# Layer two's edge pass: four row updates per step become one scan over features and columns

## The chip, the cores and the metric

The kernel runs on one core of one Trainium2 chip. The metric is the device time of one execution in microseconds (us), the median of the runs shown. A step of the work is followed on five engines: TensorE (PE, with PEld for its weight loads), VectorE (DVE), ScalarE (ACT), GpSimd (POOL) and SyncE (SP, which only issues DMAs). Each engine takes its instructions strictly in the order of the program; between engines only semaphores order anything.

## The reference, cut to what matters

Four graph layers run one after the other over 50000 nodes with 256 features and 25000 edges sorted by target node. After each layer its result is added to the node features and a layer norm is taken. The change is in the third of them, which the code calls layer two (L2): attention over the incoming edges of a node, with 8 heads of 32 features.

```python
def _L2_gnn_ref(feat, src, dst, W, attn_l, attn_r):
    ft = (feat @ W).reshape(n, H, D)
    a1 = jnp.einsum('nhd,hd->nh', ft, attn_l)
    a2 = jnp.einsum('nhd,hd->nh', ft, attn_r)
    e = jax.nn.leaky_relu(a1[src] + a2[dst], negative_slope=ALPHA)
    m = jax.ops.segment_max(e, dst, num_segments=n)
    ex = jnp.exp(e - m[dst])
    s = jax.ops.segment_sum(ex, dst, num_segments=n)
    alpha = ex / s[dst]
    msg = ft[src] * alpha[:, :, None]
    out = jax.ops.segment_sum(msg, dst, num_segments=n)
    return jax.nn.elu(out.reshape(n, H * D))
...
x = _layernorm(x + _L2_gnn_ref(x, src, dst, L2_gnn_W, L2_gnn_attn_l, L2_gnn_attn_r), axis=-1)
```

## The kernel before

The program has six phases with a barrier after each: layer zero's edges, two passes over the nodes, layer two's edge pass (the functions `e2_...`), layer three's edge pass, and a last pass over the nodes. The change touches layer two's edge pass alone.

There the sorted edges are cut into 128 runs of 196, one run per partition, and the pass goes through the runs column by column, J = 4 columns to a step, CS = 49 steps. Each partition so keeps, from column to column, a running maximum, a running sum and a running weighted mean (the row, 256 features) of the edges of its current target node; at the first edge of a new node they start afresh. Column j of a step does row = al * previous row + B, where al is one factor per head and B is the column's own message.

All loops are unrolled, and what stands where on each engine is the order of the code, written out by hand:

- **TensorE** (`e2_tensor`): for each column four transposes (L1356) of source and target features into one PSUM bank, then matmuls with the layer's weights (L1367, L1369). The transposes of a column wait for the ScalarE copy that frees their bank, two columns earlier; the matmuls wait for ScalarE's copy of their own column.
- **ScalarE** (`e2_scalar`), per step s: `ev` (L1402) copies the transposes of step s+1 out of PSUM, two columns, then `ex` (L1407, exponentials of the weights of step s), then the two other columns of `ev`; then `normed` of step s-1 (L1426, four instructions, the normalised rows that are stored), `tail` (L1412, the running sum and maximum into the row's last columns), and `relu_exp` (L1417 Relu, L1419 Exp, 1024 elements each), which needs the step's rows.
- **VectorE** (`e2_vector`), per step s: `chain(s)` (L1506 to L1526, thirteen short instructions on scores and maxima), `settle(s-1)` (L1533 to L1549: the ELU, the residual and the layer-norm statistics of the step before, which needs the Exp of `relu_exp(s-1)`), `sums_rows(s)`: the running sum, a reciprocal, the factors `cf2`; B for two columns at a time (L1565) with the factor al2 between them (L1569); then for each column al * previous row (L1578), a fill of the target features (L1582) and the sum with B (L1586). Each row waits for the row before it.
- **GpSimd** gathers source rows, scatters results, and works out the layer norm's scale (`rstd`) between them. **SyncE** loads target rows, stores the rows (`raw_store`, L1279) and the results.

So a step's rows go from VectorE to ScalarE (`relu_exp`) and back (`settle`), and ScalarE's copies `ev` go to TensorE and back.

Of the kernel before, what the change touches and what calls it, by code (L numbers as in the profile page):

```python
# [94 lines left out]
def gnn_program(nc, x, src, dst, ea256, ea64,  # L95
# [62 lines left out]
    with ctx:  # L158
# [1037 lines left out]
        def scan(v, out, a, c, op0, op1):  # L1196
# [10 lines left out]
        xT2 = take([2, 4, P])  # L1207
        row2 = take([NG, J, TW])
        un2 = take([J, D])
        rr2 = take([2, J, D])  # L1210
        y2 = take([NG, J, D])
        tB2 = take([J, D])
        adx2 = take([2, H2, J + 1])
# [7 lines left out]
        cf2 = take([2, H2, J])  # L1221
        al2 = take([H2, J])
        st2 = take([J, 6])
# [21 lines left out]
        e2 = {k: Signal(sem(f"e2_{k}")) for k in  # L1245
              ("tab", "rowd", "zero", "head", "hrow", "ev", "chain", "eL", "M", "d", "w", "s", "tail", "cf", "B", "A", "S", "xc",
               "mn", "ex", "u", "r", "nm", "end", "spread", "top", "wx", "wT", "old", "z", "wf", "new", "fix", "fixed")}
# [13 lines left out]
        def e2_sync(sp):  # L1261
# [14 lines left out]
            def raw_store(s):  # L1276
                wait(sp, e2["S"], J * (s + 1))
                wait(sp, e2["tail"], s + 1)
                sp.dma_start(raws_v[s, :, :, :], row2[:, s % NG, :, :]).then_inc(e2_rw[s % NG].sem, 16)  # L1279
# [118 lines left out]
        def e2_scalar(act):  # L1398
# [29 lines left out]

            wait(act, e2["zero"], 5)
            for j in range(J):  # L1430
                ev(0, j)
            for s in range(CS):
                for j in range(J):
                    if j == J // 2:
                        ex(s)
                    if s + 1 < CS:
                        ev(s + 1, j)
                if s > 0:
                    normed(s - 1)
                tail(s)  # L1440
                wait(act, e2["S"], J * (s + 1))
                relu_exp(s, row2[:, s % NG, :, 0:D], un2, s)
            wait(act, e2["top"], 3)
# [11 lines left out]
        def e2_vector(v):  # L1455
            t = [0]

            def link(ins):
                t[0] += 1
                ins.then_inc(e2["tab"].sem, 1)  # L1460
                wait(v, e2["tab"], t[0])
            for a in (row2[:, NG - 1, J - 1, :], adx2, ee2, ms2, ww2):
                v.memset(a, 0.0).then_inc(e2["zero"].sem, 1)
# [33 lines left out]
            v.memset(KEEP3[:, CS - 1, :, 1], 0.0).then_inc(e2["rowd"].sem, 1)  # L1497
            wait(v, e2["zero"], 5)

# [28 lines left out]
            def settle(s):  # L1528
                c, b = s % NG, s % 2
                wait(v, e2["ex"], s + 1)  # L1530
                wait(v, e2["S"], J * (s + 1))
# [19 lines left out]
            def sums_rows(s):  # L1551
                b, c = s % 2, s % NG
                w1, w2 = ww2[:, 2 * b, :, :], ww2[:, 2 * b + 1, :, :]
                sums = ms2[:, b, 0, :, :]
                wait(v, e2["w"], s + 1)
                scan(v, sums, w1, w2, ALU.mult, ALU.add).then_inc(e2["s"].sem, 1)
                wait(v, e2["s"], s + 1)
                wait(v, e2["S"], J * s)
                v.reciprocal(inv2, sums[:, :, cur]).then_inc(e2["cf"].sem, 1)
                wait(v, e2["cf"], 3 * s + 1)  # L1560
                v.tensor_tensor(out=cf2, in0=ww2[:, 2 * b:2 * b + 2, :, cur],
                                in1=inv2.rearrange("p (a h) j -> p a h j", a=1).to_broadcast([P, 2, H2, J]), op=ALU.mult).then_inc(e2["cf"].sem, 1)
# [7 lines left out]
                wait(v, e2["cf"], 3 * s + 3)  # L1570
                wait(v, e2_rw[c], 16 * (s // NG))
                if s > 0:
                    wait(v, e2["r"], s)
# [628 lines left out]
```

## Time and profile before

| | |
|---|---|
| runs | 5112.55, 5115.06, 5118.44 us; median 5115.06 us |
| profiled execution | 5112.93 us, span 5111.2 us |
| busy over the span | PE 4226.6 us (83%), DVE 3516.5 us (69%), ACT 1963.0 us (38%), POOL 3216.0 us (63%) |
| layer two's edge pass, 3274 to 3980 us | DVE busy 633.87 us of 706, PE 503.98, POOL 481.13, ACT 326.77 |
| mean granted TensorE clock | 0.904 of full speed over the span, 0.75 in this pass |

The profile is one execution. A row of the timeline gives the start and the duration of an instruction (or of several alike, merged), and in brackets how long its engine had been idle before it and what ended that. Two instructions that follow each other on an engine overlap a little, so what one costs is best read from start to start. TensorE's clock is given as a share of its higher level: 1.00 is 2.4 GHz and 0.50 is 1.2 GHz.

### The profile page before, as it was taken

The page shows a single profiled execution, that of the slowest core. Times are in us where ns is not written, and L with a number is a line of the kernel's source. Part 1 is how long each engine was busy: PE and PEld are TensorE (multiplying, and loading weights), DVE is VectorE, ACT ScalarE, POOL GpSimd, SP SyncE. Part 2 cuts the span into 40 slices and gives each one's busy share as a digit, 9 for nine tenths or more (in the row PEclk, how much of TensorE's full clock was granted, in tenths as well). Part 3 has the DMA queues.
Part 4 walks back from the last instruction along what each step waited for, and adds up shares of the span by engine and source line. Part 5 has one row for each costly group of instructions (what it writes and reads, how often), then busy time and mean ns, then how long its engine had stood idle before and what let it go on. Part 6 is the DMA issues. An engine that isn't in the chain of part 4 may idle for free. (4 is left out here: it accounts for less than half of the span.)

```text
span 5111.2 us, 69926 instructions
## 1 busy us (share of the span) xinstructions
PE 4226.6 (83%) x18336; PEld 3066.5 (60%) x18336; DVE 3516.5 (69%) x10200; ACT 1963.0 (38%) x3445; POOL 3216.0 (63%) x3078
## 2 busy tenths in 40 slices
PE   2177759998999999999999999777776687768886
PEld 1055535555666666666666666566665677756665
DVE  3055545666666666666666666599999688879998
ACT  0011115553333333333333333344444222237776
POOL 7388754444456666666655656677775677756666
PEclk6588879999999999999999999877777788889999
DMA  9988879998544444444444444355554444448886
GB/s 373 324 157 153 161 141 362 364 367 312 198 175 152 142 143 144 142 140 140 148 142 141 141 141 146 111 183 183 194 183 162 136 140 134 154 166 288 289 288 220
DMA packets 449380, 994.26 MB, mean 195 GB/s; under 512 B 147560, under 2 KB 230474, under 8 KB 449198
## 3 DMA queue, kind: packets, MB, share of 16 engines
q1 hardware_dynamic: 296146, 732.73, 42.1%
q0 software_dynamic: 100736, 172.47, 13.4%
q10 hardware_dynamic: 52316, 87.06, 5.0%
q8 instruction: 62, 1.02, 0.1%
q14 instruction: 120, 0.98, 0.1%
HBM read 493.48 MB, written 541.33 MB: 202 GB/s over the span
## 5 line engine op out<-in xcount | busy, mean ns | idle before, releaser
L1140 PE MATMUL psum<-W2b,arena 128*128 128x256 f32 x3136 | 725.2, 379 | 0.0
L1121 PE MATMUL psum<-arena,W1b 128*128 128x512 f32 x1568 | 699.1, 599 | 0.0
L1140 PEld LDWEIGHTS psum<-W2b,arena 128*128 128x128 f32 x3136 | 573.1, 190 | 66.3 <-issue 0.5
L1121 PEld LDWEIGHTS psum<-arena,W1b 128*128 128x128 f32 x1568 | 289.8, 190 | 402.8 <-issue 402.8
L1009 ACT ACTIVATE arena<-psum,hbias 128x512 f32<-128x512 f32 x392 | 269.4, 687 | 565.3 <-PE psum L1121 565.3
L1367 PE MATMUL psum<-Wg,arena 128*128 128x264 f32 x784 | 299.6, 520 | 167.5 <-ACT arena L1402 166.7
L825 DVE TENSOR_SCALAR arena<-arena 128x256 f32<-128x256 f32 x392 | 135.4, 409 | 424.8 <-POOL arena L820 424.8
L959 POOL DMA_INDIRECT xd_d<-arena,FE x360 | 356.3, 990 | 99.4 <-issue 99.4
L464 POOL DMA_INDIRECT tab<-arena x196 | 310.7, 1585 | 168.6 <-DMA tab<-zero 68.6
L816 POOL TENSOR_TENSOR arena<-arena,lneps 128x4 f32<-128x4 f32 x196 | 41.5, 212 | 549.2 <-DVE arena L812 548.3
L603 PE MATMUL psum<-arena,NEG 128*128 128x324 f32 x500 | 177.3, 521 | 245.1 <-ACT arena L409 212.5
L1097 PE MATMUL psum<-W2a,arena 128*128 128x256 f32 x1568 | 357.1, 381 | 9.3 <-ACT arena L995 9.3
L2025 PE MATMUL psum<-Wg,arena 128*128 128x256 f32 x1568 | 355.4, 380 | 0.8 <-ACT arena L2041 0.8
L1097 PEld LDWEIGHTS psum<-W2a,arena 128*128 128x128 f32 x1568 | 299.6, 191 | 92.5 <-issue 54.3
L778 PE MATMUL psum<-arena,W1a 128*128 128x512 f32 x784 | 354.1, 595 | 0.0
L728 POOL DMA_INDIRECT fe_d<-EID,FIRST x196 | 196.4, 1002 | 239.6 <-ACT arena L753 209.3
L2084 POOL TENSOR_TENSOR arena<-arena 128x1024 f32<-128x1024 f32 x98 | 230.4, 2351 | 164.1 <-DVE arena L2125 159.6
L939 POOL TENSOR_TENSOR arena<-arena,b2b 128x1024 f32<-128x1024 f32 x98 | 230.7, 2354 | 157.0 <-DVE arena L1078 154.0
L1071 DVE TENSOR_TENSOR arena<-arena 128x4 f32<-128x4 f32 x98 | 214.4, 2188 | 149.3 <-issue 146.5
L409 ACT ACTIVATE arena<-psum 128x324 f32<-128x324 f32 x196 | 71.5, 446 | 632.1 <-DMA tab<-arena 579.6
L2025 PEld LDWEIGHTS psum<-Wg,arena 128*128 128x128 f32 x1568 | 290.9, 191 | 36.8 <-ACT arena L2041 1.2
L1367 PEld LDWEIGHTS psum<-Wg,arena 128*128 128x128 f32 x784 | 182.2, 257 | 205.4 <-ACT arena L1402 178.2
(349 smaller groups left out, 10167.0 us busy)
## 6 DMA issues: line engine op xcount, KB each, us to landing
arena<-in_x SPq DMA_DIRECT2D x194, 512.0 KB, 5.4
x_d<-arena SPq DMA_DIRECT2D x194, 512.0 KB, 3.7
tab<-zero SPq DMA_DIRECT2D x11, 5832.0 KB, 54.3
arena<-x_d SPq DMA_DIRECT2D x105, 512.0 KB, 4.4
tab<-blank SPq DMA_DIRECT2D x97, 544.0 KB
arena<-tab SPq DMA_DIRECT2D x97, 544.0 KB
h_d<-arena SPq DMA_DIRECT2D x98, 512.0 KB, 4.7
arena<-h_d SPq DMA_DIRECT2D x98, 512.0 KB
```

The source lines that it names most:

```text
L464: pool.indirect_dma_start(out=tab0[:, :], out_offset=bass.IndirectOffsetOnAxis(ap=sidx[:, s, j:j + 1], axis=0), in_=comb[:, s % NC, j, :], ...
L778: last = pe.matmul(psum[:, 4 + 2 * b + g, :], W1a[:, f, g * P:(g + 1) * P], hT[:, b, f, :], start=(f == 0), stop=(f == FH - 1))
L939: pool.tensor_tensor(out=x1b[:, k.b, :, :], in0=x1[:, k.b, :, :], in1=b2b[:, :].rearrange("p (a d) -> p a d", a=1).to_broadcast([P, J, D]) ...
L959: pool.indirect_dma_start(out=xd_d[:, :], out_offset=bass.IndirectOffsetOnAxis(ap=FE[:, s * J + j:s * J + j + 1], axis=0), in_=x2[:, s % 2 ...
L1009: act.activation(hid[:, c, :], psum[:, HB[c], :], ACT.Relu, bias=hbias[:, c:c + 1]).then_inc(p3["hidr"], 1)
L1071: v.tensor_tensor(out=lone[:, 0, :], in0=lnB.mv[:, :, 1], in1=lnB.rs, op=ALU.mult).then_inc(lonely["lvar"], 1)
L1097: last = pe.matmul(outA(j), p3y[:, f, j * P:(j + 1) * P], W2a[:, f, :], start=(f == 0), stop=(f == FH - 1))
L1121: last = pe.matmul(psum[:, HB[c], :], W1b[:, f, c * P:(c + 1) * P], x1T[:, f, :], start=False, stop=(f == FH - 1))
L1140: last = pe.matmul(outB(j), hid[:, c, j * P:(j + 1) * P], W2b[:, c, :], start=(c == 0), stop=(c == KH - 1))
L1367: pe.matmul(o[:, 0:D + H2], xT2[:, j % 2, f, :], Wg[2][:, f, 0:D + H2], start=(f == 0), stop=(f == FH - 1))
L2025: done = pe.matmul(psum[:, c + j // 2, (j % 2) * D:(j % 2 + 1) * D], l_xT[:, k.slot(2), f, j * P:(j + 1) * P], Wg[3][:, f, 0:D], start=(f ...
L2084: pool.tensor_tensor(out=l_rr[:, k.slot(4), :, :], in0=l_pr[:, k.slot(2), :, :], in1=l_xt[:, k.slot(NXT), :, :], op=ALU.add).then_inc(lp[" ...
```

## The change

The four rows of a step are no longer made by eight VectorE instructions but by one scan, `tensor_tensor_scan`, over 256 features times 5 columns: along each feature it computes state = al * state + B. Column 0 holds the previous step's last row (copied there by L1582 of the new file) with the factor zero, which starts each feature afresh. Rows now lie as features x columns in a new tile run2 (two buffers, five elements = 20 bytes from one feature to the next), and B is written in that layout too. Since a scan reads a factor for every element, ScalarE spreads the 8 x 5 factors over 8 x 32 x 5 (`spread`, 1280 elements); and since the store wants rows as columns x features, ScalarE copies them back into row2 after `relu_exp` (1024 elements). `relu_exp` and `settle` read run2 with a stride of 20 bytes. The fill of the target features stays: two of its four instructions stand ahead of the scan, two behind it. `raw_store` and the pass's last row wait for ScalarE's copy (signal raw) instead of the row updates.

```diff
+            def spread(s):
+                wait(act, e2["cf"], 3 * s + 3)
+                wait(act, e2["S"], s)
+                act.activation(al5.rearrange("p (h c) j -> p h c j", h=H2), al2.rearrange("p h (a j) -> p h a j", a=1).to_broadcast([P, H2, D // H2, J + 1]),
+                               ACT.Copy).then_inc(e2["A"].sem, 1)
...
                 if s > 0:
                     normed(s - 1)
+                spread(s)
                 tail(s)
-                wait(act, e2["S"], J * (s + 1))
-                relu_exp(s, row2[:, s % NG, :, 0:D], un2, s)
+                wait(act, e2["S"], s + 1)
+                relu_exp(s, run2[:, s % 2, :, 1:J + 1].rearrange("p d j -> p j d"), un2, s)
+                wait(act, e2_rw[s % NG], 16 * (s // NG))
+                act.activation(row2[:, s % NG, :, 0:D], run2[:, s % 2, :, 1:J + 1].rearrange("p d j -> p j d"), ACT.Copy).then_inc(e2["raw"].sem, 1)
...
-                v.scalar_tensor_tensor(out=rr2[:, b, :, :], in0=un2, scalar=-1.0, in1=row2[:, c, :, 0:D], op0=ALU.add, op1=ALU.max).then_inc(e2["u"].sem, 1)
+                v.scalar_tensor_tensor(out=rr2[:, b, :, :], in0=un2, scalar=-1.0, in1=run2[:, b, :, 1:J + 1].rearrange("p d j -> p j d"), op0=ALU.add, op1=ALU.max).then_inc(e2["u"].sem, 1)
...
+                wait(v, e2["A"], s)
+                v.tensor_tensor(out=al2[:, :, cur], in0=cf2[:, 0, :, :], in1=sums[:, :, last], op=ALU.mult).then_inc(e2["cf"].sem, 1)
                 for h in range(2):
-                    v.tensor_tensor(out=tB2[:, 2 * h:2 * h + 2, :].rearrange("p j (h c) -> p j h c", h=H2),
+                    v.tensor_tensor(out=tB2[:, :, 1 + 2 * h:3 + 2 * h].rearrange("p (h c) j -> p j h c", h=H2),
...
-                    if h == 0:
-                        v.tensor_tensor(out=al2, in0=cf2[:, 0, :, :], in1=sums[:, :, last], op=ALU.mult).then_inc(e2["cf"].sem, 1)
...
+                v.tensor_copy(tB2[:, :, 0], run2[:, 1 - b, :, J]).then_inc(e2["B2"].sem, 1)
                 wait(v, e2["mm"], J * (s + 1))
                 for j in range(J):
-                    prev = row2[:, c, j - 1, 0:D] if j else row2[:, (c - 1) % NG, J - 1, 0:D]
-                    wait(v, e2["S"], J * s + j)
-                    v.tensor_tensor(out=split(row2[:, c, j, 0:D], H2), in0=split(prev, H2), in1=heads(al2[:, :, j], H2), op=ALU.mult).then_inc(e2["A"].sem, 1)
...
-                    wait(v, e2["A"], J * s + j + 1)
-                    wait(v, e2["B"], 2 * s + j // 2 + 1)
-                    v.tensor_tensor(out=row2[:, c, j, 0:D], in0=row2[:, c, j, 0:D], in1=tB2[:, j, :], op=ALU.add).then_inc(e2["S"].sem, 1)
+                    if j == 1:
+                        wait(v, e2["A"], s + 1)
+                        wait(v, e2["B"], 2 * s + 2)
+                        wait(v, e2["B2"], s + 1)
+                        wait(v, e2["raw"], s - 1)
+                        wait(v, e2["ex"], s - 1)
+                        v.tensor_tensor_scan(out=run2[:, b, :, :].rearrange("p d j -> p (d j)"), data0=al5.rearrange("p d j -> p (d j)"),
+                                             data1=tB2.rearrange("p d j -> p (d j)"), initial=0.0, op0=ALU.mult, op1=ALU.add).then_inc(e2["S"].sem, 1)
...
-            wait(v, e2["S"], J * CS)
+            wait(v, e2["raw"], CS)
```

On ScalarE, in the middle of the pass, one step before (L1402 is `ev`, L1407 `ex`, L1426 `normed`, L1412 `tail`, L1417 and L1419 `relu_exp`):

```order
L1402 ACTIVATE arena<-psum 128x512 x2
L1407 ACTIVATE arena<-arena 128x16x4
L1402 ACTIVATE arena<-psum 128x512 x2
L1426 ACTIVATE arena<-arena 128x256 x4
L1412 ACTIVATE arena<-arena 128x2x4x8
L1417 ACTIVATE arena<-arena 128x1024
L1419 ACTIVATE arena<-arena 128x1024
```

The same step of the changed kernel (L1404 is `ev`, L1409 `ex`, L1435 `normed`, L1415 `spread`, L1421 `tail`, L1426 and L1428 `relu_exp`, L1454 the copy into row2):

```order
L1404 ACTIVATE arena<-psum 128x512 x2
L1409 ACTIVATE arena<-arena 128x16x4
L1404 ACTIVATE arena<-psum 128x512 x2
L1435 ACTIVATE arena<-arena 128x256 x4
L1415 ACTIVATE arena<-arena 128x1280
L1421 ACTIVATE arena<-arena 128x2x4x8
L1426 ACTIVATE arena<-arena 128x1024
L1428 ACTIVATE arena<-arena 128x1024
L1454 ACTIVATE arena<-arena 128x4x256
```

The new `spread` stands behind all four `ev` and behind `normed`; the new copy stands between the Exp and the next step's first `ev`.

On VectorE, `sums_rows` of one step before, from the factors cf2 (L1561) to the first instructions of the next `chain` (L1506); the group L1578, L1582, L1586 comes four times in a row and is shown once:

```order
L1561 TENSOR_TENSOR arena<-arena 128x64
L1565 TENSOR_TENSOR arena<-psum,arena 128x512
L1569 TENSOR_TENSOR arena<-arena 128x32
L1565 TENSOR_TENSOR arena<-psum,arena 128x512
L1578 TENSOR_TENSOR arena<-arena 128x256
L1582 SCALAR_TENSOR_TENSOR arena<-arena,KEEP 128x256
L1586 TENSOR_TENSOR arena<-arena 128x256
...
L1506 COPY arena<-psum 128x8x2 x2
```

The same stretch of the changed kernel (L1573 is cf2, L1577 al2, L1579 the two B, L1582 the copy of the previous row, L1588 the fill of the target features, L1596 the scan, L1518 the next `chain`):

```order
L1573 TENSOR_TENSOR arena<-arena 128x64
L1577 TENSOR_TENSOR arena<-arena 128x8x4
L1579 TENSOR_TENSOR arena<-psum,arena 128x2x256 x2
L1582 COPY arena<-arena 128x256
L1588 SCALAR_TENSOR_TENSOR arena<-arena,KEEP 128x256 x2
L1596 SCALAR_TENSOR_TENSOR arena<-arena 128x1280
L1588 SCALAR_TENSOR_TENSOR arena<-arena,KEEP 128x256 x2
L1518 COPY arena<-psum 128x8x2 x2
```

The factor al2 moved ahead of both B, and the scan, which waits for ScalarE's `spread`, took the place of the eight row instructions.

## Rows read from the trace of the kernel before

**Rows 1.** Waits, 3300 to 3900 us: engine line <- releaser: total us, times, longest
```profile
ACT arena L1417 <- DVE arena L1586: 67.0, 44, 2.8
...
DVE arena L1533 <- ACT arena L1419: 18.6, 44, 0.4
```

**Rows 2.** Timeline of ScalarE, a late step: start us, us, engine, line, what [idle before]
```profile
3921.06 1.06 ACT L1417 ACTIVATE arena<-arena 128x1024 f32<-128x1024 f32 x1 [1.81 <-DVE arena L1586]
3922.14 1.06 ACT L1419 ACTIVATE arena<-arena 128x1024 f32<-128x1024 f32 x1
3923.11 1.06 ACT L1402 ACTIVATE arena<-psum 128x512 f32<-128x512 f32 x2
...
3930.17 0.60 ACT L1402 ACTIVATE arena<-psum 128x512 f32<-128x512 f32 x1 [2.07 <-PE psum L1356]
3930.66 2.06 ACT L1426 ACTIVATE arena<-arena 128x256 f32<-128x256 f32 x4
3932.63 0.30 ACT L1412 ACTIVATE arena<-arena 128x64 f32<-128x64 f32 x1
3934.76 1.06 ACT L1417 ACTIVATE arena<-arena 128x1024 f32<-128x1024 f32 x1 [1.83 <-DVE arena L1586]
```

**Rows 3.** Timeline of VectorE, one step in the middle of the pass
```profile
3512.70 1.22 DVE L1533 SCALAR_TENSOR_TENSOR arena<-arena 128x1024 f32<-128x1024 f32 x1 [0.43 <-ACT arena L1419]
...
3519.45 0.41 DVE L1578 TENSOR_TENSOR arena<-arena 128x256 f32<-128x256 f32 x1
...
3519.78 0.48 DVE L1582 SCALAR_TENSOR_TENSOR arena<-arena,KEEP 128x256 f32<-128x256 f32 x1
...
3524.10 0.25 DVE L1506 COPY arena<-psum 128x16 f32<-128x16 f32 x2
...
3525.77 0.19 DVE L1526 TENSOR_TENSOR arena<-arena,NEG 128x32 f32<-128x32 f32 x1
...
3526.39 1.23 DVE L1533 SCALAR_TENSOR_TENSOR arena<-arena 128x1024 f32<-128x1024 f32 x1 [0.43 <-ACT arena L1419]
```

**Rows 4.** Timeline of ScalarE: first and last `ev` of two early steps
```profile
3293.62 1.06 ACT L1402 ACTIVATE arena<-psum 128x512 f32<-128x512 f32 x2
...
3299.67 0.60 ACT L1402 ACTIVATE arena<-psum 128x512 f32<-128x512 f32 x1 [1.13 <-PE psum L1356]
...
3320.98 1.06 ACT L1402 ACTIVATE arena<-psum 128x512 f32<-128x512 f32 x2
...
3328.69 0.60 ACT L1402 ACTIVATE arena<-psum 128x512 f32<-128x512 f32 x1 [2.75 <-PE psum L1356]
```

**Rows 5.** Busy time by stretch: us, PE, PEld, DVE, ACT, POOL busy (instructions), PEclk, DMA
```profile
3294.20:3297.60 3.40, 3.34 (x12) 2.94 (x13) 3.33 (x6) 0.64 (x3) 0.00 (x0) 0.52 0.01 2
3297.60:3301.00 3.40, 3.00 (x19) 2.54 (x18) 3.22 (x16) 1.93 (x4) 2.27 (x3) 0.97 0.00 0
...
3325.00:3328.40 3.40, 3.40 (x14) 2.99 (x13) 3.20 (x16) 0.60 (x1) 2.26 (x3) 0.50 0.09 33
```

**Rows 6.** Groups of VectorE instructions by shape, scans: count | busy us, mean ns | idle
```profile
L1198 DVE TENSOR_TENSOR_SCAN arena<-arena 128x20 f32<-128x20 f32 x98 | 19.3, 197 | 1.7
...
L1198 DVE TENSOR_TENSOR_SCAN arena<-NEG,arena 128x40 f32<-128x40 f32 x49 | 11.8, 241 | 1.7
L1198 DVE TENSOR_TENSOR_SCAN arena<-arena 128x40 f32<-128x40 f32 x49 | 11.5, 234 | 0.3 <-ACT arena L1407 0.3
...
L1198 DVE TENSOR_TENSOR_SCAN arena<-NEG,arena 128x20 f32<-128x20 f32 x49 | 9.9, 201 | 4.4
```

**Rows 7.** Groups of ScalarE instructions by shape: count | busy us, mean ns | idle
```profile
L1417 ACT ACTIVATE arena<-arena 128x1024 f32<-128x1024 f32 x49 | 51.8, 1056 | 79.6 <-DVE arena L1586 79.6
...
L1412 ACT ACTIVATE arena<-arena 128x64 f32<-128x64 f32 x49 | 15.0, 306 | 0.0
L1801 ACT ACTIVATE arena<-arena 128x48 f32<-128x48 f32 x49 | 14.2, 289 | 85.9 <-DVE arena L1198 85.9
L1407 ACT ACTIVATE arena<-arena 128x64 f32<-128x64 f32 x49 | 12.5, 256 | 0.7 <-DVE arena L1526 0.7
```

More of the change, by code:

```diff
@@ L1208, in gnn_program @@
         row2 = take([NG, J, TW])
+        run2 = take([2, D, J + 1])
+        al5 = take([D, J + 1])
+        tB2 = take([D, J + 1])
         un2 = take([J, D])
@@ L1211, in gnn_program @@
         y2 = take([NG, J, D])
-        tB2 = take([J, D])
         adx2 = take([2, H2, J + 1])
@@ L1221, in gnn_program @@
         cf2 = take([2, H2, J])
-        al2 = take([H2, J])
+        al2 = take([H2, J + 1])
         st2 = take([J, 6])
@@ L1245, in gnn_program @@
         e2 = {k: Signal(sem(f"e2_{k}")) for k in
-              ("tab", "rowd", "zero", "head", "hrow", "ev", "chain", "eL", "M", "d", "w", "s", "tail", "cf", "B", "A", "S", "xc",
+              ("tab", "rowd", "zero", "head", "hrow", "ev", "chain", "eL", "M", "d", "w", "s", "tail", "cf", "B", "A", "S", "xc", "raw", "B2",
                "mn", "ex", "u", "r", "nm", "end", "spread", "top", "wx", "wT", "old", "z", "wf", "new", "fix", "fixed")}
@@ L1276, in raw_store @@
             def raw_store(s):
-                wait(sp, e2["S"], J * (s + 1))
+                wait(sp, e2["raw"], s + 1)
                 wait(sp, e2["tail"], s + 1)
@@ L1427, in normed @@
                                    scale=rs2[:, s % 2, j:j + 1]).then_inc(e2["y"].sem, 1)
-            wait(act, e2["zero"], 5)
+            wait(act, e2["zero"], 6)
             for j in range(J):
@@ L1461, in link @@
                 wait(v, e2["tab"], t[0])
-            for a in (row2[:, NG - 1, J - 1, :], adx2, ee2, ms2, ww2):
+            for a in (run2[:, 1, :, J], al2, adx2, ee2, ms2, ww2):
                 v.memset(a, 0.0).then_inc(e2["zero"].sem, 1)
@@ L1497, in e2_vector @@
             v.memset(KEEP3[:, CS - 1, :, 1], 0.0).then_inc(e2["rowd"].sem, 1)
-            wait(v, e2["zero"], 5)
+            wait(v, e2["zero"], 6)
             def chain(s):
@@ L1530, in settle @@
                 wait(v, e2["ex"], s + 1)
-                wait(v, e2["S"], J * (s + 1))
+                wait(v, e2["S"], s + 1)
                 wait(v, e2["y"], J * (s - 1))
-                v.scalar_tensor_tensor(out=rr2[:, b, :, :], in0=un2, scalar=-1.0, in1=row2[:, c, :, 0:D], op0=ALU.add, op1=ALU.max).then_inc(e2["u"].sem, 1)
+                v.scalar_tensor_tensor(out=rr2[:, b, :, :], in0=un2, scalar=-1.0, in1=run2[:, b, :, 1:J + 1].rearrange("p d j -> p j d"), op0=ALU.add, op1=ALU.max).then_inc(e2["u"].sem, 1)
                 wait(v, e2["u"], s + 1)
@@ L1557, in sums_rows @@
                 wait(v, e2["s"], s + 1)
-                wait(v, e2["S"], J * s)
+                wait(v, e2["S"], s)
                 v.reciprocal(inv2, sums[:, :, cur]).then_inc(e2["cf"].sem, 1)
                 wait(v, e2["cf"], 3 * s + 1)
-                v.tensor_tensor(out=cf2, in0=ww2[:, 2 * b:2 * b + 2, :, cur],
-                                in1=inv2.rearrange("p (a h) j -> p a h j", a=1).to_broadcast([P, 2, H2, J]), op=ALU.mult).then_inc(e2["cf"].sem, 1)
+                v.tensor_tensor(out=cf2, in0=ww2[:, 2 * b:2 * b + 2, :, cur], in1=inv2.rearrange("p (a h) j -> p a h j", a=1).to_broadcast([P, 2, H2, J]),
+                                op=ALU.mult).then_inc(e2["cf"].sem, 1)
                 wait(v, e2["cf"], 3 * s + 2)
+                wait(v, e2["A"], s)
+                v.tensor_tensor(out=al2[:, :, cur], in0=cf2[:, 0, :, :], in1=sums[:, :, last], op=ALU.mult).then_inc(e2["cf"].sem, 1)
                 for h in range(2):
-                    v.tensor_tensor(out=tB2[:, 2 * h:2 * h + 2, :].rearrange("p j (h c) -> p j h c", h=H2),
+                    v.tensor_tensor(out=tB2[:, :, 1 + 2 * h:3 + 2 * h].rearrange("p (h c) j -> p j h c", h=H2),
                                     in0=psum[:, pair(s, h), 0:D].rearrange("p j (h c) -> p j h c", h=H2),
                                     in1=cf2[:, 1, :, 2 * h:2 * h + 2].rearrange("p h (j a) -> p j h a", a=1).to_broadcast([P, 2, H2, D // H2]), op=ALU.mult).then_inc(e2["B"].sem, 1)
-                    if h == 0:
-                        v.tensor_tensor(out=al2, in0=cf2[:, 0, :, :], in1=sums[:, :, last], op=ALU.mult).then_inc(e2["cf"].sem, 1)
[L1570 to L1573, printed above, removed]
+                v.tensor_copy(tB2[:, :, 0], run2[:, 1 - b, :, J]).then_inc(e2["B2"].sem, 1)
                 wait(v, e2["mm"], J * (s + 1))
                 for j in range(J):
-                    prev = row2[:, c, j - 1, 0:D] if j else row2[:, (c - 1) % NG, J - 1, 0:D]
-                    wait(v, e2["S"], J * s + j)
-                    v.tensor_tensor(out=split(row2[:, c, j, 0:D], H2), in0=split(prev, H2), in1=heads(al2[:, :, j], H2), op=ALU.mult).then_inc(e2["A"].sem, 1)
                     if s or j:
@@ L1676, in gnn_program @@
         e3_end = cursor[0]
-        done2 = dict(zero=5, head=16, tr=J * CS, ev=J * CS, mm=J * CS, chain=CHAIN * CS, eL=3 * CS, M=2 * CS, d=2 * CS, w=CS, s=CS, tail=CS,
-                     cf=3 * CS, B=2 * CS, A=J * CS, S=J * CS, end=2, spread=3, top=3, wx=1, wT=1, old=16, z=2, wf=1, new=13, fix=1, fixed=32)
+        done2 = dict(zero=6, head=16, tr=J * CS, ev=J * CS, mm=J * CS, chain=CHAIN * CS, eL=3 * CS, M=2 * CS, d=2 * CS, w=CS, s=CS, tail=CS,
+                     cf=3 * CS, B=2 * CS, A=CS, S=CS, end=2, spread=3, top=3, wx=1, wT=1, old=16, z=2, wf=1, new=13, fix=1, fixed=32)
         e3 = {k: e2[k].after(n) for k, n in done2.items()}
```

## The prediction, made before the changed kernel ran

> **What bounds the kernel now.** I read the waits of the pass first, then the timelines of two engines over one step. The waits [rows 1] show how the pass hangs together: ScalarE's Relu waits 67.0 us for VectorE's rows, and VectorE's `settle` waits 18.6 us for ScalarE's Exp, 44 times each, about once a step. Both directions wait, but VectorE far less: one step, from `settle` to `settle`, is 13.69 us (3512.70 to 3526.39), and 0.43 us of it is a wait [rows 3]. VectorE sets the pace. ScalarE's step [rows 2] adds up from start to start: Relu 1.08, Exp 0.97, first to last `ev` 7.06, 0.49 for the last `ev`, `normed` 1.97, `tail` 0.30, then 1.83 idle, 13.70 in all. ScalarE looks half empty, but its own order takes 11.87 us of the 13.70 whether it is busy or not: inside the `ev` stretch it waits for TensorE's transposes (2.07 us ahead of the last `ev` alone), and whatever is written behind that waits too. That the spare time is only 1.83 us a step is what the reader is to keep from these rows.
>
> TensorE's part of that stretch changes with its clock. It took 6.05 us in an early step (3293.62 to 3299.67) and 7.71 us in another (3320.98 to 3328.69) [rows 4]. In the first, TensorE worked at a granted clock of 0.52 (about its lower level, 1.2 GHz) for one stretch of 3.4 us and then at 0.97; in the second it still stood at 0.50 while it worked through the stretch that followed [rows 5]. Ahead of both it had stood idle, waiting for ScalarE.
>
> **The change on VectorE.** Between the factors and the next `chain` the eight row instructions and the four fills take 4.65 us (3519.45 to 3524.10) [rows 3]. They become one copy, four fills and one scan. The copy has 256 elements like L1578, which is followed 0.33 us later [rows 3]: 0.33. A fill lasts 0.48 [rows 3]; each now follows the one it needs, so about 0.51 for it, 2.0 for four. The scan: from 20 to 40 elements a scan grows from 197 to 234 ns, or from 201 to 241 [rows 6], that is 1.85 to 2.0 ns an element, so 1280 elements cost 234 + 1240 x 1.85 = 2.53 us to 241 + 1240 x 2.0 = 2.72 us; I take 2.65. Sum about 4.98, less some 0.25 because instructions that don't need each other overlap by about 0.08 (0.41 long, 0.33 apart): 4.73 against 4.65. **VectorE gains nothing in its own work**: the scan alone takes 2.65 us, and the fills no longer have row instructions between them to hide their waits for each other. What it could gain is the 0.43 us wait for the Exp, since the scan ends two fills before the step's rows did.
>
> The reads and writes with a stride of 20 bytes on VectorE (1024 elements in `settle`, 1024 in the two B, 256 in the copy) cost from nothing to, at the upper price worked out below for ScalarE, 2304 x 0.78 ns = 1.8 us a step. I count them as nothing because of a wait in front of the scan, below, that covers them; without that cover they would be the 1.8 us.
>
> **The change on ScalarE.** `spread` has 1280 elements: from 64 elements (256 ns) to 1024 (1056 ns) an instruction grows by 0.83 ns an element [rows 7], so 1.27 us. The copy into row2 has 1024 elements like the Exp, which is followed 0.97 us later [rows 2]: 0.97. Relu and copy read with a stride of 20 bytes. Two instructions of the trace do that too: L1412 takes 306 ns for 64 elements, where L1407 takes 256 for as many without the stride, and L1801, the like of L1412 in layer three, takes 289 for 48 [rows 7]. If the 50 ns are a price per element (0.78 ns), 1024 elements pay 0.80 us; if they are fixed, 0.05. The step from 48 to 64 elements (17 ns for 16, 1.06 an element, 0.23 above 0.83) lies between, and gives 306 + 960 x 1.06 - 1056 = 0.27 us. I take 0.27 for each of the two and keep the ends.
>
> The Trainium skill (SBUF — State Buffer, Specifications (TRN2)) speaks against this layout: lines there are 16 bytes, and each access that crosses to a new line pays a penalty, which at 20 bytes every element would. The 50 ns of L1412 agree that something is paid; by that rule at the full price of 0.78 ns the sum is that of the second rival, by the slope it is the forecast's.
>
> **Where the new wait lies.** `spread(s)` stands behind all `ev` of step s+1 and behind `normed(s-1)`, and the scan waits for it. Before, VectorE needed ScalarE once a step (Exp to `settle`); now also in the middle, and ScalarE's next instructions (Relu, Exp, copy, then `ev`, and with it TensorE) wait for the scan. That closes a loop through the whole of ScalarE's order, which I add up from rows 2: Relu 1.08 + 0.27, Exp 0.97, copy 0.97 + 0.27, `ev` 7.06 (the latest full step's, between 6.05 and 7.71), last `ev` 0.49, `normed` 1.97, `spread` 1.27, scan 2.65, and 0.03 for each of two hand-overs (the Exp starts 1.08 after a Relu of 1.06 that it needs). Sum 17.06 us. `tail` drops out, as it runs beside the scan.
>
> Does VectorE come later than that? After the scan it has two fills (0.95 with the overlap) and `chain` (3524.10 to 3525.96, 1.86 us [rows 3]), so `settle` starts 2.8 us after the Relu; from `settle` to where the copy stands is 6.75 us (3512.70 to 3519.45), and copy and two fills bring the scan to 8.1: 10.9 us after the Relu. The spread factors are there at 14.35. So VectorE waits about 3.4 us a step in front of the scan, more than the 1.8 us of strides could fill. Queued behind that wait on VectorE are two fills and the next `chain`; `ex` on ScalarE needs the latter only about 1.7 us after it is done, and loads and stores on SyncE and GpSimd stay steps ahead. `normed` doesn't wait for GpSimd in rows 2, and it now starts 1.5 us later after the Relu, while `settle`, which GpSimd's scale comes from, starts 0.6 later, so it won't. TensorE's longer idle time leaves it no reason to run faster than before.
>
> So a step goes from 13.69 to 17.06 us, +3.37. The pass has 49 steps and 48 intervals. In the last there is no `ev`, and the wait shrinks: I take +1.2 (between 0 and 3.4). At the end the last row waits for Relu, Exp and copy, 1.35 + 0.97 + 1.3 = 3.6 us that were not ahead of it. 47 x 3.37 + 1.2 + 3.6 = 163 us. The profiled execution took 5112.93 us (span 5111.2), 2.1 below the median of 5115.06; 5112.93 + 163 = 5276, and on the median **5278 us**.
>
> **The rivals.**
>
> *VectorE stays the bound (the other side).* If the factors were there when VectorE reaches the scan, 8.1 us after `settle`, a step would be 13.69 - 0.43 + 0.08 = 13.34 us: 5115 - 48 x 0.35 + 3.6 = 5102 us. It decides from the point where ScalarE's order is 3.4 us shorter than I add up. The shortest TensorE stretch gives 1.0 of that [rows 4] and strides at no price 0.5; nothing gives the other 1.9. Against it stands every row of ScalarE's order; for it only that ScalarE is idle much of the time. The Trainium skill (VectorE: DVE Perf Modes, Rules for kernel authors) says to minimise the number of chained VectorE instructions; by that rule alone, eight for one, the change would end here.
>
> *Strided reads at full price.* Relu and copy cost 0.80 us more each instead of 0.27: 18.12 a step, 47 x 4.43 + 5 = 213, 5328 us. For it: L1412's 50 ns per 64 elements; against it: L1801 with 48 elements shows nearly as much.
>
> *TensorE's stretch at its ends.* With 6.05 us in each step, 47 x 1.01 = 47 us less: 5231. With 7.71, 47 x 0.65 = 31 more: 5309. A new step length can put TensorE's rise in clock elsewhere in the step, and the rows show both. The scan's ends (2.53, 2.72) move the sum by 6 us at most.
>
> **How the numbers follow.** The loop as added up, with TensorE's stretch anywhere between its ends, 5231 to 5309: 0.75. Strides at full price: 0.17. VectorE as bound: 0.04. Something slower than now but under 5231, as a TensorE stretch shorter than any here: 0.04. The predicted time is the first case's, 5278. The range 5230 to 5330 takes in the first two. A measurement of this kernel can tell some 0.2% (10 us) from no change. Faster by more than that is most of the VectorE case, 0.03; within it 0.02; slower 0.95.
>
> **What would show it.** In the changed kernel's trace: the scan with an idle time of about 3.4 us (1.5 if VectorE's strides cost) in front of it, ended by ScalarE's `spread`, some 160 us in all; the scan at 2.5 to 2.75 us; `settle` no longer waiting for the Exp; ScalarE's Relu and copy at 1.1 to 1.3 us (1.85 in the second rival), no idle time ahead of `spread`, and steps of about 17 us against 13.69. It would be wrong if `spread` started well before `normed` ended its wait for TensorE, if the scan took half the time, or if the wait stood in front of another instruction, `settle` or `chain`.

## The result, and the profile after

The changed kernel takes **5359.96 us** (median of 4 runs, 5351.18 to 5363.05) against 5113.81 us (4 runs, 5112.01 to 5118.44) of the kernel before on the same chip: ratio 1.0482, 95% interval 1.0469 to 1.0495. It is slower, as forecast, but by 246 us where 163 were forecast: 5278 was 82 us too low, and the range ended at 5330. The profiled execution of after took 5351.18 us (span 5349.4); against the 5112.93 of the one before that is 238 us, and it is what the traces below have to account for.

The waits of the changed kernel, 3300 to 4100 us (engine, line <- releaser: total us, times, longest us); they answer to [rows 1]:

```profile
PE psum L1369 <- ACT arena L1404: 378.2, 43, 8.8
...
DVE arena L1596 <- ACT arena L1415: 136.7, 43, 3.9
ACT arena L1426 <- DVE arena L1596: 115.4, 43, 2.7
DVE arena L1545 <- ACT arena L1428: 20.6, 43, 0.5
```

L1415 is `spread`, L1596 the scan, L1426 the Relu, L1428 the Exp, L1545 `settle`. The new wait is there, in front of the scan, 3.18 us each time (136.7 / 43). But the old wait of `settle` for the Exp is there too, 0.48 us each time; it should have gone.

ScalarE's timeline over one step of after (start us, us, engine, line, what, [idle before]), which answers to [rows 2]:

```profile
3514.18 2.03 ACT L1426 ACTIVATE arena<-arena 128x1024 f32<-128x1024 f32 x1 [2.69 <-DVE arena L1596]
3516.24 1.06 ACT L1428 ACTIVATE arena<-arena 128x1024 f32<-128x1024 f32 x1
3517.20 2.03 ACT L1454 ACTIVATE arena<-arena 128x1024 f32<-128x1024 f32 x1
3519.14 1.07 ACT L1404 ACTIVATE arena<-psum 128x512 f32<-128x512 f32 x2
...
3525.79 0.60 ACT L1404 ACTIVATE arena<-psum 128x512 f32<-128x512 f32 x1 [1.66 <-PE psum L1358]
3526.28 2.06 ACT L1435 ACTIVATE arena<-arena 128x256 f32<-128x256 f32 x4
3528.25 1.25 ACT L1415 ACTIVATE arena<-arena 128x1280 f32<-128x1280 f32 x1
...
3532.39 2.04 ACT L1426 ACTIVATE arena<-arena 128x1024 f32<-128x1024 f32 x1 [2.68 <-DVE arena L1596]
```

From Relu to Relu it is the forecast's loop, link by link, with nothing in it that was not in the sum: 2.06 for the Relu, 0.96 Exp, 1.94 copy (L1454), 6.65 from first to last `ev`, 0.49, 1.97 `normed`, 1.29 `spread`, 2.85 scan. Two links stand out. **Relu and copy run 2.03 us, as long again as the Exp between them, which has as many elements** and reads them in a row.

VectorE in the same step, which answers to [rows 3]:

```profile
3511.32 2.83 DVE L1596 TENSOR_TENSOR_SCAN arena<-arena 128x1280 f32<-128x1280 f32 x1 [3.86 <-ACT arena L1415]
...
3517.33 2.00 DVE L1545 SCALAR_TENSOR_TENSOR arena<-arena 128x1024 f32<-128x1024 f32 x1 [0.46 <-ACT arena L1428]
...
3523.65 2.01 DVE L1579 TENSOR_TENSOR arena<-psum,arena 128x512 f32<-128x512 f32 x2
3525.49 0.41 DVE L1582 COPY arena<-arena 128x256 f32<-128x256 f32 x1
...
3529.54 2.82 DVE L1596 TENSOR_TENSOR_SCAN arena<-arena 128x1280 f32<-128x1280 f32 x1 [2.77 <-ACT arena L1415]
```

`settle` takes 2.00 us where it took 1.22 [rows 3], and VectorE, with that and the longer B's (L1579), comes to the copy 8.16 us after `settle` starts, against 6.75 before. It still waits 2.77 us for the factors there.

Groups by line and shape over the whole execution (count | busy us, mean ns | idle us before them), which answer to [rows 7] and [rows 6]:

```profile
L1426 ACT ACTIVATE arena<-arena 128x1024 f32<-128x1024 f32 x49 | 100.0, 2041 | 131.6 <-DVE arena L1596 131.6
L1454 ACT ACTIVATE arena<-arena 128x1024 f32<-128x1024 f32 x49 | 99.6, 2034 | 0.0
...
L1596 DVE TENSOR_TENSOR_SCAN arena<-arena 128x1280 f32<-128x1280 f32 x49 | 138.4, 2824 | 150.3 <-ACT arena L1415 150.3
```

The steps of after are not alike. Most take 18.2 and 19.3 us in turn, because TensorE's stretch from first to last `ev` is short and long in turn: the step before the one shown has 7.75 us (3499.82 to 3507.57) where this one has 6.65. Busy time over these two stretches (us; PE, PEld, DVE, ACT, POOL busy with instructions; PEclk; DMA):

```profile
3499.82:3507.57 7.75, 7.09 (x25) 6.27 (x26) 7.36 (x22) 1.83 (x5) 4.50 (x5) 0.51 0.10 31
3519.14:3525.79 6.65, 6.02 (x25) 5.33 (x26) 6.40 (x21) 1.80 (x5) 2.25 (x3) 0.60 0.00 0
```

The two stretches hold as many matmuls, and TensorE is idle for about 0.65 us in each. What differs is the granted clock: 0.51 on average over the long one, almost all of it at the lower level (1.2 GHz), and 0.60 over the short one, in which it rises sooner. TensorE had stood idle for ScalarE ahead of both, as ahead of the stretches of [rows 5], but longer: 8.8 us a step by the first of the waits above (378.2 / 43). Over the 47 steps the stretch lasts 6.09 to 7.76 us, 7.09 on average.

**Where the time went:** the 47 steps average 18.65 us (first Relu 3289.59) against 13.69, 47 x 4.96 = 233 us. The last interval is 2.4 us longer, the end from the last Relu to the next pass's first 5.9 longer, and the first Relu is 2.0 earlier: 239 us in all, for the 238 to account for.

### The profile page after: what moved, and what is told of

The parts are those of the page before. It is cut to its first block and busy times, and to the rows that moved or that the text cites. A ratio compares the mean times of both kernels' runs of the same rounds, so it can differ in the third digit from the quotient of the medians.

```text
span 5349.4 us, 69678 instructions
## 1 busy us (share of the span) xinstructions
PE 4202.8 (79%) x18336; PEld 3051.3 (57%) x18336; DVE 3600.5 (67%) x9907; ACT 2163.2 (40%) x3543; POOL 3329.4 (62%) x3078
## 5 line engine op out<-in xcount | busy, mean ns | idle before, releaser
L1369 PEld LDWEIGHTS psum<-Wg,arena 128*128 128x128 f32 x784 | 182.1, 257 | 448.7 <-ACT arena L1404 422.3
L603 PE MATMUL psum<-arena,NEG 128*128 128x324 f32 x500 | 159.4, 479 | 234.1 <-ACT arena L409 201.5
L1309 POOL DMA_INDIRECT x_d<-arena,IDX x196 | 284.5, 1452 | 62.2 <-issue 51.8
```

The lines of the kernel that those rows point to most:

```text
L1309: pool.indirect_dma_start(out=x3_d[:, :], out_offset=bass.IndirectOffsetOnAxis(ap=IDX[:, 2, c:c + 1], axis=0), in_=y2[:, s % NG, j, :], in ...
L1369: pe.matmul(o[:, 0:D + H2], xT2[:, j % 2, f, :], Wg[2][:, f, 0:D + H2], start=(f == 0), stop=(f == FH - 1))
```

## The experiments

**What a stride costs by itself.** Behind the end of the changed kernel, with nothing else running, ScalarE copies and VectorE sums of 1024 elements, one after the other (lines shortened; the signals between them are left out).

```diff
+ for k in (1, 2, 3, 4, 5, 6, 8): act.activation(o, src(k)[:, :, 0], ACT.Copy)
+ act.activation(o, src(5)[:, 0:256, 1:5], ACT.Copy)
+ act.activation(os, src(1)[:, :, 0], ACT.Copy)
+ act.activation(os, src(5)[:, :, 0], ACT.Copy)
+ for k in (1, 2, 3, 4, 5): v.tensor_tensor(out=o, in0=src(k)[:, :, 0], in1=src(1)[:, :, 0], op=ALU.add)
+ v.tensor_tensor(out=o, in0=src(5)[:, :, 0], in1=src(5)[:, :, 0], op=ALU.add)
+ v.tensor_tensor(out=os, in0=src(1)[:, :, 0], in1=src(1)[:, :, 0], op=ALU.add)
...
+ v.tensor_tensor_scan(out=..., data0=arena[:, 0:640], ...)
```

`src(k)` reads each k-th float, `os` is written at each fifth.

> The changed kernel with a stretch of single instructions behind its end, on data of no meaning, to price strides by themselves: ten ScalarE copies of 1024 elements (read at strides of 1, 2, 3, 4, 5, 6 and 8 elements; read in runs of 4 out of 5; written at stride 5; both at stride 5), eight VectorE sums of 1024 elements (first input at strides 1 to 5, both at 5, output at 5, input and output at 5), and scans of 640 and 1280 elements. If the 2.04 us of Relu and copy in the changed kernel is the stride alone, the copy at stride 5 takes 2.04 us here, with nothing beside it, and the sum with one input at stride 5 takes 2.00 against 1.22. If it is a collision with VectorE's fills that run beside it, stride 5 takes 1.06. If the price comes with an element's own 16-byte line, strides 4 to 8 cost the same and runs of 4 nearly nothing; if with any stride over one, stride 2 costs it already. Scan: 2.82 us at 1280 and 1.48 at 640 if it is a price per element.

Timeline of that stretch (columns as above): L2182 to L2188 read at 1, 2, 3, 4, 5, 6 and 8 floats; L2189 four of every five; L2190 writes at 5; L2191 reads and writes at 5; L2206 to L2210 sum with one input at 1 to 5; L2211 both inputs at 5; L2212 the output at 5; L2214 is a scan of 640.

```profile
5364.84 1.06 ACT L2182 ACTIVATE arena<-arena 128x1024 f32<-128x1024 f32 x1 [12.89 <-DVE arena L2203]
5365.93 1.12 ACT L2183 ACTIVATE arena<-arena 128x1024 f32<-128x1024 f32 x1
5367.08 1.56 ACT L2184 ACTIVATE arena<-arena 128x1024 f32<-128x1024 f32 x1
5368.67 2.01 ACT L2185 ACTIVATE arena<-arena 128x1024 f32<-128x1024 f32 x1
5370.71 2.02 ACT L2186 ACTIVATE arena<-arena 128x1024 f32<-128x1024 f32 x1
...
5374.79 2.04 ACT L2188 ACTIVATE arena<-arena 128x1024 f32<-128x1024 f32 x1
5376.86 1.06 ACT L2189 ACTIVATE arena<-arena 128x1024 f32<-128x1024 f32 x1
5377.95 2.02 ACT L2190 ACTIVATE arena<-arena 128x1024 f32<-128x1024 f32 x1
5380.00 2.02 ACT L2191 ACTIVATE arena<-arena 128x1024 f32<-128x1024 f32 x1
5382.12 1.23 DVE L2206 TENSOR_TENSOR arena<-arena 128x1024 f32<-128x1024 f32 x1 [17.37 <-ACT arena L2191]
...
5384.64 1.51 DVE L2208 TENSOR_TENSOR arena<-arena 128x1024 f32<-128x1024 f32 x1
...
5388.19 1.97 DVE L2210 TENSOR_TENSOR arena<-arena 128x1024 f32<-128x1024 f32 x1
5390.19 1.98 DVE L2211 TENSOR_TENSOR arena<-arena 128x1024 f32<-128x1024 f32 x1
5392.20 1.98 DVE L2212 TENSOR_TENSOR arena<-arena 128x1024 f32<-128x1024 f32 x1
...
5396.22 1.49 DVE L2214 TENSOR_TENSOR_SCAN arena<-arena 128x640 f32<-128x640 f32 x1
```

With nothing beside it the copy takes 2.02 us at stride 5 and 1.06 in a row, 0.94 ns more an element (0.96 / 1024). So the 2.03 us of Relu and copy is the stride's alone, not contention. On ScalarE half the price is due at 3 floats, all of it from 4 on, none in runs of four. VectorE pays 0.74 us for one strided operand and no more for two.

The Trainium skill (SBUF — State Buffer, Specifications (TRN2)) has lines of 16 bytes, of which each needs at least two hits for full bandwidth, and a penalty for each access that crosses to a new one. ScalarE's rows agree. At 2 floats every line is hit twice, and the copy takes 1.12 us; at 3 floats, 12 bytes, two of every four elements are alone in their line, and half the price is due (0.50 us); from 4 floats on each element is alone, and 5 cost no more than 4. In runs of four out of five each line is hit at least three times, and nothing is due.

**The extra work on ScalarE alone.** The kernel before, with an instruction like `spread` that nobody waits for; and with one like the copy as well.

```diff
                     normed(s - 1)
+                act.activation(dum5, KEEP[...], ACT.Copy)
                 tail(s)
```

> The kernel before with one more ScalarE instruction where the change puts the spreading of factors, a copy of 1280 elements into a tile that nobody reads; no wait is added. Loop theory (the cost is the wait of the scan for an instruction late in ScalarE's order): the 1.2 us fit into the 1.4 to 2.8 us that ScalarE waits for VectorE's rows each step, so 5114, the same within 5 us. Load theory (ScalarE can't bear more work beside TensorE's copies): up to 1.16 x 48 = 56 us more, 5170.

Measured 5110.43 us against 5110.44 (ratio 1.0002, interval 0.9992 to 1.0011). The 1.2 us a step cost nothing, as the 1.83 us of spare time [rows 2] said.

```diff
                 relu_exp(s, row2[:, s % NG, :, 0:D], un2, s)
+                act.activation(dumr, zero[:, :], ACT.Copy)
```

> The kernel before with both of the change's ScalarE instructions as dead weight: the copy of 1280 elements behind the layer norm, and a copy of 1024 elements (contiguous) behind the Exp, into tiles that nobody reads. No wait is added and VectorE is as before. Loop theory: ScalarE's order grows from 11.87 to some 14.0 us a step against 13.69, so only 0.3 us a step and 15 us in all, 5129, up to 5150 if TensorE's stretch is at its long end. Load theory: most of the 246 us that the change cost, over 5250.

Measured 5110.53 us against 5110.44 (1.0003, 0.9994 to 1.0012): again nothing, which I had not expected, as ScalarE's order adds up to 14.0 us with both. ScalarE's timeline in that kernel (L1442 and L1446 are the added ones, L1419 the Relu):

```profile
3507.52 1.26 ACT L1442 ACTIVATE arena<-KEEP 128x1280 f32<-128x1280 f32 x1
...
3509.02 1.06 ACT L1419 ACTIVATE arena<-arena 128x1024 f32<-128x1024 f32 x1
...
3511.07 1.04 ACT L1446 ACTIVATE arena<-zero 128x1024 f32<-128x1024 f32 x1
3512.01 1.06 ACT L1404 ACTIVATE arena<-psum 128x512 f32<-128x512 f32 x2
...
3518.72 0.60 ACT L1404 ACTIVATE arena<-psum 128x512 f32<-128x512 f32 x1 [1.72 <-PE psum L1358]
```

The idle time ahead of the Relu is gone, and TensorE's stretch is 6.71 us (3512.01 to 3518.72), where the same step of the kernel before has 7.50 (3512.58 to 3520.08): the mean granted clock in it is 0.60 against 0.54. So what the change adds to ScalarE, at these unstrided lengths, costs nothing as work. What it costs has to come by the waits or by the strides.

**The wait alone, the strides alone, neither.** Three kernels and the change itself make one table. `e_early` writes `spread` five instructions earlier in ScalarE's program, ahead of the last `ev` and the four of `normed`; nothing else differs from the change.

```diff
                 for j in range(J):
...
+                    if j == J - 1:
+                        spread(s)
                     if s + 1 < CS:
                         ev(s + 1, j)
                 if s > 0:
                     normed(s - 1)
-                spread(s)
```

> The changed kernel with the spreading of factors one place earlier in ScalarE's order: ahead of the last of the four copies out of PSUM (ev), where ScalarE waits for TensorE anyway, and so ahead of the layer norm's four instructions too. Nothing else differs, not one instruction more or less. Loop theory: the scan no longer waits for ScalarE (about 3.2 us a step less), a step is some 15.5 us against 18.65, 5360 - 48 x 3.15 = 5209. Rival, that the change costs by its strides and its added work alone: same instructions, so 5360.

Measured 5200.31 us (5198.16 to 5202.87), ratio 1.0177 (1.0159 to 1.0196); steps of 15.40 us. The scan there (groups by line and shape):

```profile
L1597 DVE TENSOR_TENSOR_SCAN arena<-arena 128x1280 f32<-128x1280 f32 x49 | 138.1, 2817 | 0.0
L1546 DVE SCALAR_TENSOR_TENSOR arena<-arena 128x1024 f32<-128x1024 f32 x49 | 98.1, 2002 | 24.5 <-ACT arena L1428 24.5
```

The wait of 150.3 us is gone to nothing, and 160 us of time with it. `settle` still waits 0.5 us a step for the Exp.

`x_flat_late` is the change with every access of those tiles in a row (the same elements in number, at other places), `spread` where the change has it.

```diff
- relu_exp(s, run2[:, s % 2, :, 1:J + 1].rearrange("p d j -> p j d"), un2, s)
+ relu_exp(s, flat2(run2[:, s % 2, :, :])[:, D:D * (J + 1)].rearrange("p (j d) -> p j d", j=J), un2, s)
```

The copy, `settle`, both B's and the copy of the last column are rewritten alike.

> The same without strides, but with the factors spread where the change has them, behind all ev and the layer norm. The values land in other places here too. This is the loop of the forecast with no price for strides: 1.08 + 0.97 + 0.97 + 7.08 + 0.49 + 1.97 + 1.30 + 2.85 = 16.7 us a step, (16.7 - 13.69) x 47 + 5 = 146 more, 5256, up to 5273 if TensorE's stretch is nearer its long end. If the wait costs only together with the strides: near 5111.

Measured 5274.34 us (5270.57 to 5276.95) against 5113.72, ratio 1.0315 (1.0298 to 1.0332).

```profile
L1599 DVE TENSOR_TENSOR_SCAN arena<-arena 128x1280 f32<-128x1280 f32 x49 | 138.5, 2826 | 169.9 <-ACT arena L1418 169.9
L1548 DVE SCALAR_TENSOR_TENSOR arena<-arena 128x1024 f32<-128x1024 f32 x49 | 59.5, 1214 | 0.0
```

This comes closest to the kernel that was forecast, though the forecast had 0.54 us a step for strides: the scan waits 3.5 us a step (169.9 / 49; forecast 3.4), `settle` no longer waits, the time is 4 us from 5278. Of this run's own expectation it is the upper end.

`x_flat` has both edits.

> The changed kernel without any stride, and with the factors spread ahead of the last ev: B, the copy of the previous row, Relu, the copy into row2 and settle use the two tiles as if they lay columns x features, contiguous, while the scan still runs over all 1280 elements in order. So the rows are not the layer's (the values land in other places), and the time is that of the idea with wait and strides taken out. If VectorE gains nothing by the scan but the wait for the Exp: 13.34 and 0.17 for the scan's true 2.82, 13.5 a step, some 5107, within 0.3% of 5111. Rival, that the scan would be a clear gain if only its layout were free: under 5080.

Measured 5098.71 us (5095.16 to 5101.09), ratio 0.9970 (0.9961 to 0.998); steps of 13.32 us on average. Neither the scan nor `settle` waits:

```profile
L1600 DVE TENSOR_TENSOR_SCAN arena<-arena 128x1280 f32<-128x1280 f32 x49 | 138.1, 2818 | 0.0
...
L1549 DVE SCALAR_TENSOR_TENSOR arena<-arena 128x1024 f32<-128x1024 f32 x49 | 59.9, 1222 | 0.0
```

| | `spread` late | `spread` early |
|---|---|---|
| strided | 5360 (the change) | 5200 |
| in a row | 5274 | 5099 |

The place of `spread` is worth 160 to 176 us, the strides 86 to 102, each give or take the 3 us by which the kernel before differs from one set of runs to the next (5110.4 to 5113.8). With neither the change gains 15 us: it is the VectorE-bound rival, 13.34 us a step and 5102 us by its sum.

**Which strides.** `e_runs` lets Relu and copy read the scan's tile in its own order, in runs of four; the copy then writes at a stride, and `settle` has two strided operands for one. `e_early_runs` is that with `spread` early.

```diff
- un2 = take([J, D])
+ un2 = take([D, J])
- relu_exp(s, run2[:, s % 2, :, 1:J + 1].rearrange("p d j -> p j d"), un2, s)
+ relu_exp(s, run2[:, s % 2, :, 1:J + 1], un2, s)
- act.activation(row2[:, s % NG, :, 0:D], run2[...].rearrange("p d j -> p j d"), ACT.Copy)
+ act.activation(row2[:, s % NG, :, 0:D].rearrange("p j d -> p d j"), run2[...], ACT.Copy)
```

> The changed kernel with Relu and the copy into row2 going through run2 feature by feature, in runs of four adjacent elements, in place of column by column at 20 bytes: un2 is kept as features x columns, so that settle reads two operands with a stride; the copy writes row2 with a stride of a row. The spreading of factors stays where it is. If the stride of the reads is the mis-sized term: Relu 2.04 to 1.06 us, and the copy too if ScalarE's strided writes are free: 2 x 0.98 x 47 = 92 less, 5268; if strided writes cost like reads, 46 less, 5314. The scan still waits about 3 us for the spread factors.

Measured 5279.39 us (5277.27 to 5282.38), ratio 1.0332 (1.0314 to 1.0351).

```profile
3513.19 1.06 ACT L1426 ACTIVATE arena<-arena 128x1024 f32<-128x1024 f32 x1 [2.68 <-DVE arena L1596]
...
3515.24 1.97 ACT L1454 ACTIVATE arena<-arena 128x1024 f32<-128x1024 f32 x1
3517.01 1.10 ACT L1404 ACTIVATE arena<-psum 128x512 f32<-128x512 f32 x2
...
3523.66 0.60 ACT L1404 ACTIVATE arena<-psum 128x512 f32<-128x512 f32 x1 [1.60 <-PE psum L1358]
...
3530.26 1.06 ACT L1426 ACTIVATE arena<-arena 128x1024 f32<-128x1024 f32 x1 [2.69 <-DVE arena L1596]
```

The Relu is short again and the copy, which writes at the stride, is not. Still a step is 17.07 us (3513.19 to 3530.26), just as in `x_flat_late`, whose copy takes 1.04 us:

```profile
3511.56 1.06 ACT L1429 ACTIVATE arena<-arena 128x1024 f32<-128x1024 f32 x1 [2.69 <-DVE arena L1599]
...
3514.56 1.06 ACT L1407 ACTIVATE arena<-psum 128x512 f32<-128x512 f32 x2
...
3522.02 0.60 ACT L1407 ACTIVATE arena<-psum 128x512 f32<-128x512 f32 x1 [2.47 <-PE psum L1361]
...
3528.63 1.06 ACT L1429 ACTIVATE arena<-arena 128x1024 f32<-128x1024 f32 x1 [2.69 <-DVE arena L1599]
```

TensorE's stretch is 6.65 us in the first and 7.46 in the second: it takes up the 0.8 us by which the copy differs. The two stretches, `e_runs` first:

```profile
3517.01:3523.66 6.65, 5.97 (x25) 5.28 (x26) 6.40 (x19) 1.85 (x6) 3.82 (x4) 0.61 0.12 37
```

```profile
3514.56:3522.02 7.46, 6.83 (x25) 6.01 (x26) 7.17 (x22) 1.80 (x6) 4.01 (x6) 0.53 0.11 33
```

Again it is the same number of matmuls at another granted clock, 0.61 against 0.53. So the copy's stride, 0.8 us a step, cost only 5 to 8 us in all (5279 against 5274; 168.7 above the kernel before against 160.6). Taking away the Relu's stride was worth 81 (5360 against 5279), 74 in the profiled executions: 47 x 0.98 = 46 us of the Relu itself, 47 x 0.43 = 20 of TensorE's stretch (6.66 on average for 7.09), and 47 x 0.16 = 8 of the copy (the first `ev` follows 1.76 us behind its start for 1.92). The expectation for this case, 5314, left the stretch as it was and was 35 us too high.

> Both: factors spread ahead of the last ev, Relu and copy in runs. Loop theory: ScalarE's order is then about 13 us or less and VectorE binds with its own work: 13.34 and its strides, 0.78 for the two B and 0.78 for settle, 0.78 more if a second strided operand costs too: 14.9 to 15.7 a step, 5175 to 5210. It would not come back to 5114, since VectorE gained nothing by the scan. Rival, that without wait and ScalarE strides the change is a gain: under 5110.

Measured 5171.48 us (5169.05 to 5174.9), ratio 1.0121 (1.0103 to 1.014), steps of 14.85 us, neither the scan nor `settle` waiting. That is VectorE's own work: 13.32 us of `x_flat` and 1.5 of strides; the 0.55 us a step to `e_early` are mostly the wait for the Exp. Without the cover of the wait, VectorE's strides cost 1.5 us a step, 5171 against 5099; the forecast had set 1.8 for that case.

**The idea without the layout.** All that the scan has to gain on VectorE is the 0.43 us for which `settle` waits for the Exp [rows 3]. The kernel before can have that by two Relu halves, the first of which starts two rows earlier (lines shortened; signals and their waits are left out).

```diff
- wait(act, e2["S"], J * (s + 1))
- relu_exp(s, row2[:, s % NG, :, 0:D], un2, s)
+ for h in range(2):
+     wait(act, e2["S"], J * s + 2 * h + 2)
+     act.activation(un2[:, 2 * h:2 * h + 2, :], row2[:, s % NG, 2 * h:2 * h + 2, 0:D], ACT.Relu, scale=-1.0)
+ act.activation(un2, un2, ACT.Exp, scale=-1.0)
```

> The kernel before with the Relu in two halves, columns 0 and 1 as soon as these rows are there, so that only half a Relu and the Exp are left behind the last row. Tests that VectorE sets the pace before and its only loss is the 0.43 us in which settle waits for the Exp: that wait goes, 48 x 0.43 = 20 us, 5093. If ScalarE or TensorE is as close behind, less than half of that.

Measured **5093.23 us** (5092.12 to 5095.65, 7 runs) against 5110.44, ratio 0.9968 (0.9957 to 0.9979). `settle` no longer waits:

```profile
3503.12 1.22 DVE L1537 SCALAR_TENSOR_TENSOR arena<-arena 128x1024 f32<-128x1024 f32 x1
```

It beats both kernels, and is about as fast as the scan freed of both its costs (5099).

## Why the prediction was wrong in size

- **The mechanism was right.** The loop through ScalarE's whole order closes where the forecast put it, the wait stands in front of the scan, and VectorE gains nothing in its own work: `x_flat`, with neither the wait nor the strides, gains 15 us, and `b_split` gets as much without a scan.
- **The term that failed is the stride of Relu and copy.** I took 0.27 us for each, from the slope between 48 and 64 elements; it is 0.98 (2.04 against 1.06). Over 47 steps, 2 x 0.71 us are 67 of the 75 us by which the profiled execution (5351) exceeds its forecast (5276). The slope was the wrong reading: 16 elements apart, it rests on a difference of 17 ns between two instructions of different layers, and a few ns in either move it severalfold. Set against unstrided instructions of their own size the same rows gave the price: L1412's excess was 50 ns for 64 elements, and L1801's, against 256 - 16 x 0.83 = 243 ns for 48, is 46 ns, 0.96 an element [rows 7]. I had counted L1801 as evidence against the price per element, and it was the better evidence for it.
- **The second rival was the case, and its price was still low.** Its 18.12 us a step, with 2 x 0.18 more for the strides and 0.17 more for the scan, give 18.65, the measured mean. Its bound of 0.80 came from L1412 alone, so the range ended at 5330 where the full price led to 5351 in the profiled execution.
- **The scan** took 2.82 us, above my upper bound of 2.72. The scans of 640 and 1280 give 2.08 ns an element (1.33 / 640), where those of 20 and 40 had given 1.85 to 2.0.
- **`settle` still waits for the Exp.** The scan does end two fills early, but the Relu's stride delays the Exp by 1 us, and the 0.5 us is back. In `x_flat_late` and `e_runs`, with a short Relu, it is gone, as forecast.
- **VectorE's strides** cost 0.78 us in `settle` and 0.78 in the two B's, and were hidden by the wait, as the forecast had it; the wait stayed at 3.2 us, where 1.5 was forecast for that case, because ScalarE's strides lengthened the other side by nearly as much (2 x 0.71).
- **TensorE's stretch** was right on average (7.09 for 7.06), but by luck: 7.06 was the last of a series that fell from 7.71 in the kernel before, and the changed kernel has short stretches (6.1 to 6.7) and long ones (7.4 to 7.8). The last interval and the end were taken at 1.2 and 3.6 us and came to 2.4 and 5.9, 3.5 us in all, of which 2.0 came back by an earlier first Relu.
- **The sum was right for a kernel without strides** (17.06 a step, 5278; `x_flat_late` 17.07 in the step shown, 5274), but in part by errors that cancel: without the 2 x 0.27 for strides, and with `ev` 0.4 and the scan 0.2 longer.

That the wait is most of the cost, and the strides the rest, and not ScalarE's added work, was argued before and is now shown (`b_spread_copy`, `e_early`, `x_flat`). TensorE's stretch makes up for a longer copy in one kernel and is short and long in turn in another because the granted clock rises sooner or later in it (0.61 and 0.60 on average in the short ones, 0.53 and 0.51 in the long ones). What sets that moment is not settled: no run here controls it.

## What to carry to other kernels

When two engines in program order begin to wait for each other at a second place in a loop, add up the whole order between the two waits, idle time included, and look first at what stands between the producer's inputs and the producing instruction: a place five instructions earlier in ScalarE's program was worth 160 us here. Price a strided operand by its excess over a contiguous instruction of the same size, not by a slope between two small ones, and set it against what the layout saves before the layout is changed. When a rewrite cuts instructions but not the busy time of the engine that sets the pace, name the wait that it removes (here 0.43 us a step) and try to remove that alone.

## What the runs showed of the hardware

- ScalarE and VectorE pay 0.7 to 1.0 us per 1024 floats once an operand's elements lie 4 or more floats apart (ScalarE, 4 to 8 floats, 2.00 to 2.04 against 1.06 us; VectorE, 4 and 5, 1.97 against 1.23), half of it on ScalarE at 3 (1.56; VectorE 1.51), next to none at 2 (1.12). Writing costs as much as reading (2.02), two or more strided operands no more than one (1.98), runs of four nothing (1.06).
- A scan of 1280 floats takes 2.82 us, 2.08 ns an element, where a sum of 1024 takes 1.23, some 1.07 ns an element beyond the 0.41 us of 256 (L1578 in [rows 3]). The Trainium skill (DVE: opcode table, instruction layouts, handler registers and perf-mode slots, Datapath and trigger behaviour) says that the scan runs at half throughput; these rows agree.
- The same matmuls between first and last `ev` kept TensorE busy for 5.97 us at a mean granted clock of 0.61, 6.02 at 0.60, 6.83 at 0.53 and 7.09 at 0.51, and the stretch lasted 6.65, 6.65, 7.46 and 7.75 us. So steps of 17.07 us came out alike from ScalarE orders 0.8 us apart.
